# Gated attention for chosen pairs of token and head: dense halves replaced by 62 gathered blocks

## The reference

```python
s = sigmoid(x @ Ws)                       # (b, t, 8)
vals, idx = top_k(s, 3)
scores = zeros_like(s).at[bi, ti, idx].set(vals)
q, k, v = heads(x @ Wq), heads(x @ Wkv)   # 8 heads of 64
attn = softmax(einsum('bhid,bhjd->bhij', q * 64 ** -0.5, k))
out = einsum('bhij,bhjd->bhid', attn, v)
proj = einsum('bhtd,hde->bhte', out, Wo) + bo[None, :, None, :]
y = einsum('bhte,bth->bte', proj, scores) # five of eight heads are weighed by 0
```

## Time and profile before

| | us |
|---|---|
| median of 3 runs | 1144.85 |
| lowest and highest run | 1143.57, 1145.23 |
| span of the profiled execution, first to last instruction | 1141.7 |
| gated stage, from its first instruction to the narrow stage's | 157.6 to 572.0 |
| of it: lead, loop, tail | 32.5, 372.8, 9.1 |

### The profile page before, as it was taken

The page is one execution under the profiler, slowest core; times in us unless marked ns, Lnnn a source line. Parts: engine busy times, 40 slices in busy tenths (PEclk is TensorE's granted clock), DMA queues, the critical chain, the costliest instruction groups (busy, mean ns, idle before and its releaser), DMA issues. The chain is left out here.

```text
span 1141.7 us, 18915 instructions
## 1 busy us (share of the span) xinstructions
PE 1072.7 (94%) x7019; PEld 539.2 (47%) x7019; DVE 893.9 (78%) x1565; ACT 715.4 (63%) x1221; POOL 411.5 (36%) x265
## 2 busy tenths in 40 slices
PE   5599999999999999999989999999999999999997
PEld 3256765445454444554423222222222267888885
DVE  8968477766666677667788999999999268787777
ACT  6324566444344464434277888888888778888875
POOL 1047521967778776877522100000010011221201
PEclk9599999999999999999999999999999999999999
DMA  4000100000000000100011110000010013122001
GB/s 100 1 1 3 38 1 1 2 11 1 1 2 2 1 2 10 48 29 1 2 46 37 35 43 29 16 21 23 15 21 1 1 38 107 63 77 89 38 38 37
DMA packets 30915, 29.44 MB, mean 26 GB/s; under 512 B 10912, under 2 KB 26536, under 8 KB 29800
## 3 DMA queue, kind: packets, MB, share of 16 engines
q1 hardware_dynamic: 30392, 28.04, 8.3%
q10 hardware_dynamic: 432, 0.20, 0.1%
HBM read 23.57 MB, written 4.26 MB: 24 GB/s over the span
## 5 line engine op out<-in xcount | busy, mean ns | idle before, releaser
L1426 POOL TENSOR_TENSOR lead_room<-lead_room 128x1024 f32<-128x1024 f32 x112 | 269.3, 2404 | 117.3 <-ACT lead_room L1687 108.8
L2176 ACT ACTIVATE narrow_att_probs<-psum 128x512 f32<-128x512 f32 x512 | 264.6, 604 | 51.5 <-PE psum L2092 51.3
L2214 DVE TENSOR_REDUCE front_maxima<-psum 128x1 f32<-128x1024 f32 x240 | 281.4, 1218 | 14.6 <-PE psum L1189 9.9
L1687 ACT ACTIVATE lead_room<-psum 128x1024 f32<-128x1024 f32 x128 | 124.1, 1021 | 152.3 <-PE psum L1572 152.3
L1782 DVE TENSOR_REDUCE gated_maxima<-psum 128x1 f32<-128x512 f32 x256 | 164.4, 684 | 44.1 <-PE psum L1463 42.7
L2092 PE MATMUL psum<-narrow_att_q,narrow_att_k 50*128 50x512 bf16 x448 | 146.8, 384 | 3.8 <-ACT narrow_att_probs L2176 3.3
L1189 PE MATMUL psum<-narrow_att_k,narrow_att_q 48*128 48x512 bf16 x448 | 132.6, 381 | 9.5 <-DVE front_maxima L2214 2.6
L2105 PE MATMUL psum<-narrow_att_probs,narrow_att_v_ones 128*32 128x512 f32 x1024 | 136.4, 605 | 0.1
L2700 DVE TENSOR_TENSOR moe_hidden_lo<-moe_hidden,moe_hidden_hi 128x512 fp32r<-128x512 f32 x144 | 104.4, 751 | 39.0 <-ACT moe_hidden_hi L2602 38.5
L1585 PE MATMUL psum<-lead_room,gated_values 128*64 128x512 f32 x512 | 132.1, 610 | 0.0
L2598 ACT ACTIVATE moe_hidden<-psum,back_up_bias 128x512 f32<-128x512 f32 x144 | 96.2, 690 | 32.9 <-PE psum L73 32.0
(11 more groups left out here) (405 smaller groups left out, 1911.1 us busy)
## 6 DMA issues: line engine op xcount, KB each, us to landing
moe_mixb<-moe_mix_scratch SPq DMA_DIRECT2D x8, 1024.0 KB, 5.1
narrow_parts_scratch<-gated_values SPq DMA_DIRECT2D x12, 128.0 KB, 2.2
narrow_parts_scratch<-narrow_att_part SPq DMA_DIRECT2D x12, 128.0 KB, 2.1
narrow_att_q<-narrow_parts_scratch SPq DMA_DIRECT2D x14, 96.0 KB
narrow_att_q<-narrow_parts_scratch SPq DMA_DIRECT2D x42, 32.0 KB
narrow_att_k<-narrow_parts_scratch SPq DMA_DIRECT2D x14, 96.0 KB
narrow_att_k<-narrow_parts_scratch SPq DMA_DIRECT2D x42, 32.0 KB
X<-in_L_attn_inputs SPq DMA_DIRECT2D x4, 256.0 KB, 4.1
```

What stands on the lines that cost most here:

```text
L1426: pool.tensor_tensor(tally[:, n % 2, :, :], probs[:, kt % 4, :, :], so_far, ALU.add).then_inc(tallied, 1)
L1687: act.activation(probs[:, k % 4, :, :], psum[:, 2 * e:2 * e + 2, :], ACT.Exp, scale=SCALE).then_inc(exped, 1)
L2176: act.activation(probs[:, k % 3, 2 * e + u % 2, :], psum[:, SCORE_BANK + j % 3, :], ACT.Exp, scale=SCALE).then_inc(exped, 1)
L2214: dve.tensor_reduce(maxima[:, n % 2, at:at + 1], chunk.rearrange("p a b -> p (a b)"), AX.X, ALU.max).then_inc(chunk_used, 1)
```

## The change

The attention is no longer made for all tokens of a head, but for the pairs of token and head that are chosen, sorted by head. Each head's list is padded to whole blocks of 128 pairs. A batch has 3 x 1024 pairs, so 31 blocks (`BLOCKS`) hold them whatever the lists' lengths are. Two blocks are handled together: 31 pairs of blocks (`PAIRS`).

- **Lead.** Queries of all 16 token tiles, keys of all heads (transposed, by 512 tokens) and the 16 value tiles are projected from UH, UL in three passes and stored to DRAM: queries as rows of one token and head (64 fp32), keys as one record a head (64 x 1024) with that head's Wo behind it (64 x 128), values as one record a head (128 x 512). The keys of batch 1 are projected in pair 0.
- **Routing.** For each batch VectorE makes 44 steps (`step`): sigmoid, rank of each head, chosen, the position of each pair in its head's list (running sums and TensorE products with ones and with a triangle, "pos"), the block in which a head starts, and, by a TensorE product of one-hot matrices over 24 tiles ("table"), for every block and row which query row it is, and where its result goes. The head of each block goes to `places`.
- **Pair loop.** GpSimd gathers 2 x 128 query rows from DRAM by an indirect DMA each, six pairs ahead. SyncE reads the two heads from `places` into registers and loads their key and value records (rings of 5 and 3). TensorE turns the queries, makes plain fp32 scores with the queries on the output partitions, two heads side by side by rows; VectorE takes the maximum of 1024 (negated), ScalarE the exponential with the maximum as bias and the denominator as its accumulated output. TensorE turns the exponentials in 16 transposes of 128x128, ScalarE and VectorE copy two banks each, TensorE mixes (two heads side by side by columns) and multiplies with Wo out of the key record; ScalarE scales by the inverse denominator, and GpSimd scatters 2 x 128 rows of 128 to DRAM.
- **Home.** When a batch's rows are all scattered, SyncE loads them (1024 x 3 x 128), and VectorE adds three rows, each times its gate, to each token of X: batch 0 in pairs 19 and 20, batch 1 in the narrow stage (units 18 and 21).
- **Seams.** Batch 0's statistics, turn, projections and maxima for the narrow stage stand at pairs 20 to 32 (`JOBS`), eight maxima a pair. In the narrow stage batch 1's statistics, normalisation and projections move from its beginning and units 3 to 28 to units 24 to 56. Semaphores are cleared by GpSimd in the flow stage and in the narrow stage too. The three bank ring (banks 4 to 6) is kept; bank 7 holds the mix.

```diff
-    H, DH, TOPK, G = 8, 64, 3, 2
-    PAIRS = H // G
-    GROUPS = BATCH * PAIRS
-    HALVES = 2 * GROUPS
+    H, DH, TOPK, BLOCKS = 8, 64, Home.TOPK, Home.BLOCKS
+    PAIRS = BATCH * BLOCKS // 2
+    Q_RING, K_RING, V_RING, AHEAD = 8, 5, 3, 6
...
+        JOBS = {0: [("K", x, g) for x in (2, 3) for g in range(4)],
+                1: [("bturn", 0)], 2: [("bias", 0)], 3: [("pos", 1)], 4: [("bturn", 1)], 5: [("bias", 1)], 8: [("table", 1)],
+                9: [("bturn", 2)], 10: [("bias", 2)], 11: [("bturn", 3)], 12: [("bias", 3)],
+                23: [("fturn", 0)], 24: [("fturn", 1)], 25: [("fproj", 0), ("fproj", 1)], 26: [("fproj", 2), ("fproj", 3)], 27: [("fvalue", 0), ("fvalue", 1)]}
...
+            def load_k(p):
...
+                for e, h in enumerate(heads_of(p)):
+                    sp.dma_start(k_ring[e * DH:(e + 1) * DH, p % K_RING, :],
+                                 k_dram[bass.ds(h, 1)].rearrange("a d n -> (a d) n")).then_inc(k_loaded[p % K_RING], 16)
...
+                    pool.indirect_dma_start(q_rows[:, p % Q_RING, e, :], None, q_dram[b],
+                                            bass.IndirectOffsetOnAxis(ap=from_row[:, b, i:i + 1], axis=0)).then_inc(gathered[p % Q_RING], 16)
...
+                    pool.indirect_dma_start(home.rows[b], bass.IndirectOffsetOnAxis(ap=to_row[:, b, i:i + 1], axis=0),
+                                            y[:, p % Home.RING, e, :], None).then_inc(home.scattered[b][p % Home.RING], 16)
...
+            for p in range(AHEAD):
+                gather(p)
+            for p in range(PAIRS):
+                if p + AHEAD < PAIRS:
+                    gather(p + AHEAD)
+                scatter(p)
...
+            for j in range(PAIRS + 2):
+                if j < PAIRS:
+                    score(j)
+                if j == 0:
+                    for e in JOBS[0]:
+                        entry_of(e)
+                if j + 1 < PAIRS:
+                    entry_of(("q", j + 1))
+                if 1 <= j <= PAIRS:
+                    entry_of(("T", j - 1, 0))
+                    entry_of(("T", j - 1, 1))
+                if j >= 2:
+                    mix(j - 2, 1)
+                if 1 <= j <= PAIRS:
+                    entry_of(("T", j - 1, 2))
+                    entry_of(("T", j - 1, 3))
+                if j >= 2:
+                    entry_of(("Y", j - 2, 0))
+                    entry_of(("Y", j - 2, 1))
+                if 1 <= j <= PAIRS:
+                    mix(j - 1, 0)
+                if j:
+                    for e in JOBS.get(j, []):
+                        entry_of(e)
...
-            FRONT_AT = {3: "turn", 10: "first", UNITS + 4: "value", UNITS + 12: "second"}
+            FRONT_AT = {31: "turn", 38: "first", 48: "value", 56: "second"}
+            ADD_AT, STATS_AT, CENTER_AT = {18: 0, 21: 1}, {24: PERB, 25: PERB + 1}, 29
```

More of the change, by code:

```diff
@@ new lines, in _ @@
+            for t in range(STILES):
+                store_q(t)
+            store_v(0)
+            for g in range(H // 2):
+                store_k(0, g)
+            for p in range(2):
+                load_k(p)
+            store_v(1)
+            load_v(0)
+            for t in range(STILES, TILES):
+                store_q(t)
+            for p in range(2, K_RING):
+                load_k(p)
+            for g in range(H // 2):
+                store_k(1, g)
+            front.load_weights(sp)
@@ L1630, in _, with release, project_rows @@
-            for e in range(2):
-                mix(HALVES * CHUNKS - 1, e)
-            for job in tail:
-                small([job])
-                fill(pe, C, psum[:, 0, :], {("nshift",): 4, ("den", HALVES - 1): 6}.get(job, 0))
+            def release(e):
+                if previous[e] is not None:
+                    wait_taken(pe, previous[e])
+                return psum[:, bank_of(e), :]
+            def project_rows(e, hi, lo):
+                bank = release(e)
+                wait_turned(pe, e[1] // PER_Q)
+                split_product(pe, bank, UH[:, tile(e[1])], UL[:, tile(e[1])], hi, lo).then_inc(made, 1)
@@ new lines, in project_keys, with logits @@
+            def project_keys(e):
+                _, x, g = e
+                bank = release(e)
+                wait_turned(pe, x)
+                split_product(pe, bank, wqk_hi[:, 1, tile(g)], wqk_lo[:, 1, tile(g)], UH[:, quarter(x)], UL[:, quarter(x)]).then_inc(made, 1)
+            def logits(e):
+                bank = release(e)
+                pe.wait_ge(ws_loaded, 16)
+                for x in range(PERB):
+                    wait_turned(pe, PERB * e[1] + x)
+                for s, u in enumerate((UH, UL)):
+                    for x in range(PERB):
+                        last = pe.matmul(bank[32 * x:32 * x + 32, :], ws_raw[:, :], f32(u[:, quarter(PERB * e[1] + x)]), start=(s == 0),
+                                         stop=(s == 1), skip_group_check=True)
+                last.then_inc(made, 1)
@@ L1742, in _ @@
+            take(("turn", 0))
             lead.own_center(dve, 2)
@@ L1858, in narrow_attention_phase @@
-def narrow_attention_phase(nc, psum, X, C, io, front, back):
+            take(("turn", 1))
+            lead.own_center(dve, 3)
+            steps(0, range(0, 2))
+            for q in range(PERB, QUARTERS):
+                dve.wait_ge(lead.x_ready, q - PERB + 1)
+                norm.quarter_stats(dve, q)
+            lead.center(dve, 2)
+            steps(0, range(2, 9))
+            lead.center(dve, 3)
+            steps(0, range(9, 18))
+            take(("turn", 2))
+            steps(0, range(18, 25))
```

1277 lines of the change are left out of this document (723 added, 554 removed), and 3 rows, old and new, of the table LEAD.

## The result

The changed kernel takes 1126.12 us (median of 4 runs, 1121.09 to 1128.24) against 1144.51 for the kernel before beside it: a ratio of 0.984, 95% interval 0.981 to 0.986. It is faster by 18.4 us where 84 were forecast, and lies above the top of the range, 1120. The profiled execution took 1121.09. The page after: span, busy time, granted clock in 40 slices.

The account below looks back on a forecast made before the run. TensorE was taken to bound the gated attention: 205 + 220 + 56 = 481 against 572.0, -91, and +6.7 in VectorE's next stage make -84.3 from 1141.7, so 1057; plus 3.15, 1060 us, range 1030 to 1120.

Parts of the forecast that it names:

- first score: Lead before the pair loop: first score product at about 205 us against 190.1, +15, bounds +8 and +25.
- 31 pairs, plain price: Gated attention's pair loop: 31 pairs of blocks at 7.1 us each, 220 us.
- beside the pairs: Extras in the gated stage: bias, second batch's routing, returned rows, next layer's work and maxima, last pairs; 56 us.
- next stage opens: End of the gated attention stage: 481 us against 572.0, a gain of 91.
- next stages longer by: Stage after the gated attention, bound by VectorE: 24 additions at 0.28 us add 6.7; starting statistics only move.
- TensorE per pair: Pair loop: scores, transposes, mix and output products sum to 6.8 us, bounds 6.5 and 8.7.
- Rival (a): Mix in the pair loop: weight loads show, 8.7 us a pair, +50, 1110 us; chance 0.10.
- Rival (b): Pair loop: GpSimd's indirect transfers bind; no gain left at 2.46 us each, 1249 us at 3.3; chance 0.10.
- rival (c): Pair loop: transfers run at 107 GB/s, not at the ceiling, 12.2 us a pair, 1218 us; chance 0.04.
- so I add 0.3 for handing over: Pair loop: 0.3 us added to 6.8 because the score, maximum, exponential chain of 6.3 is just under it; 7.1.
- Rival (d): Pair loop: score, maximum, exponential chain not overlapped with the rest, 1 us more a pair, 1091 us; chance 0.18.
- GpSimd under 5 us a pair: Expected sign in the profile after: GpSimd busy under 5 us a pair in the pair loop.

Follow-up runs that it names:

- e17_noadd: Changed kernel with the next stage's additions of batch 1's returned rows to X left out, gated stage unaltered: 1092.97 us (ratio 0.956).
- unaltered: The changed kernel itself without any follow-up edit; its profiled execution took 1121.09 us.
- c1_late: Changed kernel with batch 1's queries stored earlier, returned rows loaded a pair earlier, next layer's maxima a pair later, routing steps ahead of maxima: 1070.35 us (0.936).
- e0_same: The changed kernel run again with nothing altered, as yardstick for the other follow-up kernels: 1127.52 us (ratio 0.984).
- e7_fill: Changed kernel plus three idle TensorE products of 512 columns per pair ahead of the output projection: 1126.22 us (ratio 0.985).
- the four edits: Against the changed kernel: batch 1's queries stored earlier, returned rows a pair earlier, next layer's maxima a pair later, routing steps ahead of maxima; together 1070.35 us.
- sets 1 and 2: First two follow-up groups: the changed kernel unaltered, and with reordered stores, loads, maxima or mix, plain last writes, or idle products: 1115.40 to 1138.77 us.
- set 3: Third follow-up group, changed kernel without later gathers, without scatters, without both, or with GpSimd's turn later: 1098.80, 1114.21, 1098.27, 1136.77 us.
- e9_plain: Changed kernel with each scatter replaced by two plain SyncE transfers of the same bytes, gathers kept: 1114.21 us (ratio 0.974).
- e10_shift: Changed kernel with GpSimd's scatters and gathers started only after the second half of the next pair's mix: 1136.77 us (ratio 0.993).
- sets 4 and 5: Last two follow-up groups, changed kernel with plain query loads, gathers first, routing first, loads or additions left out, or edits combined: 1070.35 to 1104.26 us.

## Why the prediction was wrong

The forecast of 1060 was a span of 1057.4 and 3.15; the profiled span is 61.9 longer. (An execution's time is 1.8 above its span, 1121.09 against 1119.3. The other 1.3 of the 3.15 were the spread of the runs before.) By the terms of the sum, with the stage without lag (`e17_noadd`) between (us):

| term | forecast | without lag | unaltered, profiled |
|---|---|---|---|
| first score | 205 | 216.9 | 217.9 |
| 31 pairs, plain price | 220 (7.1) | 215.5 (6.95) | |
| beside the pairs | 56 | 78.4 | |
| next stage opens | 481 | 510.8 | 533.5 |
| next stages longer by | 6.7 | | 16.1 |

The 78.4 is 510.8 - 216.9 - 215.5 = 78.4.

- **TensorE per pair: right.** 6.95 where nothing comes late (forecast 6.8 and 0.3). Rival (a) falls, the mix costs its 2.2. Rival (b) falls at 1.0 us an indirect transfer, with 2.46 as its point; rival (c) too, 322 GB/s stand in one window of `c1_late` (208.7 to 240). The rule of the Trainium skill (SBUF — State Buffer, section "SBUF: two separate sides") that I weighed against the row: in this trace it shows once, the scatter of 3.40 us. Beside VectorE's steady work, which reads PSUM, the transfers took 1.0.
- **The step that failed most: "so I add 0.3 for handing over".** With the lag the stage is 22.7 us longer (533.5 - 510.8, 1.0 of it ahead of the first score), and 30.7 in `e0_same`. Rival (d) had the size, 1 us a pair, but not the mechanism: TensorE waits for the copy of the mixed values, not for exponentials. I had assumed that a product's signal comes when the product is done; the updates above show it held for up to 3.9 us (274.65 to 278.57 in `e0_same`). What holds it is open.
- **First score 205: 11.9 too early.** I wrote that a query tile "waits for the store of an earlier one (landing 2.2)" and took the landing alone, not the place of that store in SyncE's queue behind the 2 MB.
- **Beside the pairs, 56: 22.4 too little.** From the intervals of `e17_noadd`, each less 6.95: bias 7.3 (forecast 6); batch 1's routing 9.2 (5); rows home 8.3 (8, but 6.3 of it is the wait for the transfer); next layer 7.7 (9); maxima and the end 40.6 (13 + 15), with 5.2 waiting for the stacked parts and 5.2 from the last scatter to the next stage; pair 0 with batch 1's keys 5.3 (nothing).
- **The next stage, 6.7: 9.4 too little.** Its exponentials take 14.2 us longer in the changed kernel (346.4) and 340.5 - 332.2 = 8.3 longer with the additions left out. So the additions cost about 6, as forecast; "its starting statistics only move" was the error. They and the projections moved from the start into the stretch where VectorE sets the pace. That these two make the 8.3 is argued from their place; no run took them out.
- **The price of the low clock** was no term. It follows the waits: the clock is full in the windows of `e7_fill` and `e17_noadd`. It carries part of the lag's price: over pairs 3 to 28 the scores take 7.1 us more than 1.99 each in the changed kernel's trace and 1.1 in `e17_noadd`.
- **GpSimd under 5 us a pair: right** (four at 1.0). No gather released the query transpose late and no maxima set the pace.

A check of the whole, an estimate across sets: `e17_noadd` with its additions is 1092.97 + 346.4 - 340.5 = 1099, which the range would have held; the four edits bring it to 1070, 10 above the forecast.

**Open.** Why TensorE's signals are held. In the result's runs and in sets 1 and 2 every kernel has the lag. In set 3 the two kernels whose gathers go on have it (`e9_plain` less, `e10_shift` at the scores), and the two without are free of it once the gathers are over. In sets 4 and 5 none has it, six kernels with gathers among them. So gathers take part and are not enough. Sets 2 and 5 ran on the same chip, so the chip alone isn't it; `e17_noadd` has the same gated stage, so the stage's instructions aren't either. What is left is something that differs from one program to the next, from one loading of it, or from one set to the next. That split by sets means that no edit of sets 4 and 5 is shown to have removed the lag. The unaltered kernel loaded again beside `e17_noadd` would tell these apart; it was not run.

## What to carry to other kernels

Price a queue, not an instruction: for each buffer that must come free, find the place of its store in the issuing queue and add what stands ahead of it, and put an operation that frees a shared bank ahead of longer work on its engine. Work that is called "moved" costs its full time where its engine sets the pace. And before an edit's gain is believed, run the unaltered kernel in the same set and compare stage by stage: here a stage with the same instructions was 23 to 31 us shorter in another kernel of another set. Where waiters start late, look at the times of the semaphore updates too: they tell late work from a late signal.

## What the hardware showed unexpectedly

- TensorE's results released their waiters 1.24 us after the first record of a mix half of 1.09 in some kernels, and 1.7 to 3.0 in others with the same instructions; up to 4.1 us after a transpose. The semaphore updates of several products were held and came together, six within 0.35 us.
- An indirect transfer of 128 rows takes GpSimd 0.97 to 0.99 us and 0.30 to the next, whether its rows have 256 or 512 bytes; beside a VectorE comparison from SBUF one took 3.40.
- GpSimd's DRAIN at the end of the stage ended 5.0 us after the issue of the last scatter (505.56 to 510.52), though the rows had landed after 1.3 (506.82). The next stage opened 5.2 us behind the scatter in ten of the kernels; where TensorE had more to do than that, as in `c1_late`, the drain cost nothing.
